# Ternary quantisation with interleaved groups on VectorE alone, and keys copied ahead

## What is computed

```
def _L0_attn_ref(x, Wq, Wk, Wv, Wo, lambda_init):      # 16 heads of 128
    q1, q2 = (q[..., :HHD], q[..., HHD:]); k1, k2 = (k[..., :HHD], k[..., HHD:])
    attn1 = softmax(causal(q1 k1^T * SCALE)); attn2 = softmax(causal(q2 k2^T * SCALE))
    out = (attn1 - lam * attn2) @ v
    return out.reshape(b, t, H * HD) @ Wo

def ternary_quant(w_fp32, g=64):
    w = w_fp32.astype(jnp.bfloat16)
    w_g = w.reshape(-1, g)
    scale = jnp.clip(jnp.mean(jnp.abs(w_g), axis=-1, keepdims=True), 1e-08, None)
    q = jnp.clip(jnp.round(w_g / scale), -1, 1)
    w_hat = (q * scale).reshape(w.shape)
    return w + jax.lax.stop_gradient(w_hat - w)

def _L0_ffn_ref(x, w_gate_up, w_proj):                 # 4096 x 512 and 512 x 2048
    gate, up = jnp.split(x @ ternary_quant(w_gate_up).T, 2, axis=-1)
    return rms_norm(silu(gate) * up) @ ternary_quant(w_proj).T
```

## Time and profile before

| | before |
|---|---|
| median of 3 runs | 1418.46 us (1415.54 to 1429.39) |
| span of the profiled execution | 1416.6 us |
| PE, PEld busy in it | 1114.3 us (79%), 825.4 us (58%) |
| DVE, ACT, POOL busy in it | 764.6, 469.9, 479.1 us (54%, 33%, 34%) |
| mean granted TensorE clock | 0.805 of full speed |

### The profile page before, as it was taken

How to read it: one execution, slowest core, us unless ns; L and a number is a source line. 1 busy time by engine, 2 the same in 40 slices (tenths; PEclk the granted TensorE clock), 3 DMA queues, 4 the chain that set the end, 5 groups by cost and what they waited for, 6 DMA issues and landing times.

```text
span 1416.6 us, 14414 instructions
## 1 busy us (share of the span) xinstructions
PE 1114.3 (79%) x5107; PEld 825.4 (58%) x5111; DVE 764.6 (54%) x1025; ACT 469.9 (33%) x719; POOL 479.1 (34%) x331
## 2 busy tenths in 40 slices
PE   3899977879999887686769689699733478489996
PEld 2543454547777766575657678544521367378885
DVE  6212122653344554998999995414697764533333
ACT  2111122552111634464446533333311132133331
POOL 5231212330000433465646560034454980011211
PEclk9799986975555897788878889899955555599999
DMA  6576601220000114313231300102030000111110
GB/s 174 204 266 215 253 0 28 58 60 19 0 0 1 56 42 157 117 47 119 74 106 58 125 10 16 60 0 74 15 121 0 0 0 1 48 60 44 59 44 30
DMA packets 50448, 97.88 MB, mean 69 GB/s; under 512 B 6796, under 2 KB 26564, under 8 KB 47838
## 3 DMA queue, kind: packets, MB, share of 16 engines
q1 hardware_dynamic: 47198, 86.59, 18.4%
q0 software_dynamic: 3200, 10.62, 2.2%
HBM read 96.14 MB, written 1.05 MB: 69 GB/s over the span
## 4 chain that ended last, share of the span: by engine, by line
PE 58%; DVE 23%; issue 11%; ACT 4%; POOL 2%; SPq 0%; DMA 0%; POOLq 0%; DVEq 0%; ACTq 0%
PE banks L41 7%; PE banks L42 7%; PE banks L43 7%; PE banks L354 6%; PE banks L1794 4%; PE banks L1097 3%; PE banks L1096 3%; PE banks L2109 2%; PE banks L1424 2%; PE banks L1452 2%; DVE da_a L1357 1%; PE banks L1087 1%; PE banks L1806 1%; DVE da_s L1351 1%; DVE da_s L1341 1%
## 5 line engine op out<-in xcount | busy, mean ns | idle before, releaser
L155 POOL TENSOR_TENSOR w_low<-w_raw,w_high 128x1024 fp32r<-128x1024 f32 (+2 forms) x66 | 129.9, 1982 | 307.9 <-ACT w_high L151 307.8
L354 PE MATMUL banks<-cs_rows,cs_col 128*2 128x512 f32 x192 | 85.3, 594 | 0.2 <-DVE w_raw L318 0.2
L1642 POOL TENSOR_TENSOR tw_abs<-tw_abs,tw_w 128x2048 bf16<-128x2048 bf16 x12 | 49.0, 4083 | 95.0 <-DVE tw_abs L1635 95.0
L151 ACT CAST w_high<-w_raw 128x1024 fp32r<-128x1024 f32 (+2 forms) x66 | 53.4, 831 | 83.2 <-DMA w_raw<-in_L_attn_Wq 47.1
L2217 POOL TENSOR_TENSOR hf_hl<-hf_h,hf_hh 128x512 fp32r<-128x512 f32 x16 | 20.6, 1289 | 155.1 <-ACT hf_hh L2271 155.1
L1424 PE MATMUL banks<-da_k,da_q 64*128 64x128 f32 x256 | 35.7, 396 | 38.4 <-issue 38.4
L1424 PEld LDWEIGHTS banks<-da_k,da_q 64*128 64x128 f32 x256 | 33.9, 288 | 41.5 <-issue 41.5
L41 PE MATMUL banks<-da_xT_high,w_high 128*128 128x512 f32 x128 | 52.5, 410 | 6.3 <-POOL w_low L155 5.7
L929 DVE SCALAR_TENSOR_TENSOR wa_s<-banks,wa_bd 128x288 f32<-128x288 f32 x16 | 7.3, 457 | 86.4 <-PE banks L1097 86.4
L41 PE MATMUL banks<-hf_xhh,w_high 128*128 128x512 f32 x128 | 51.7, 404 | 0.0
L669 POOL TENSOR_TENSOR wa_kr<-wa_kr,wa_tab 128x288 f32<-128x288 f32 x8 | 6.4, 794 | 132.8 <-ACT wa_kr L724 132.5
(11 more groups left out here) (419 smaller groups left out, 3160.7 us busy)
## 6 DMA issues: line engine op xcount, KB each, us to landing
cs_rows<-in_ctx SPq DMA_DIRECT2D x16, 1536.0 KB
tw_raw<-in_L_ffn_w_gate_up SPq DMA_DIRECT2D x32, 256.0 KB, 3.7
w_raw<-in_L_xattn_W_o SPq DMA_DIRECT2D x8, 512.0 KB
w_raw<-in_L_attn_Wq SPq DMA_DIRECT2D x8, 512.0 KB
w_raw<-in_L_attn_Wk SPq DMA_DIRECT2D x8, 512.0 KB
w_raw<-in_L_attn_Wv SPq DMA_DIRECT2D x8, 512.0 KB
w_raw<-in_L_attn_Wo SPq DMA_DIRECT2D x8, 512.0 KB
tw_raw<-in_L_ffn_w_proj SPq DMA_DIRECT2D x16, 256.0 KB, 3.8
```

Of the source, the lines that this page charges most:

```text
L151: self.nc.scalar.copy(self.wh[k][:, 0:cols], self.raw[k][:, 0:cols]).then_inc(self.split_hi[k], 1)
L155: self.nc.gpsimd.tensor_tensor(self.wl[k][:, 0:cols], self.raw[k][:, 0:cols], self.wh[k][:, 0:cols].bitcast(F32), ALU.subtract).then_inc(s ...
L354: ins = nc.tensor.matmul(out, self.col[:, h * self.HALF + r, :], self.rows[h][:, r, :], start=(h == 0 and r == 0), stop=False)
L1642: g.tensor_tensor(a, a, self.w[j][:, :], ALU.subtract).then_inc(self.d_ok, 1)
```

## The change

There are three parts.

1. The groups are interleaved. Within each quarter of a tile (512 elements, 8 groups of 64) the element k of group g goes to place 8 k + g. The cast on ACT writes it that way (reading on, writing with a step of 8 elements, 16 bytes). The broadcast then has its zero step in the middle and 8 neighbouring bf16 values innermost. The sum over a group reads with a step of 16 bytes. As the contracted features are now in another order, LayerNorm writes xn in that order for this block (a step of 32 bytes), and tw.out of w_gate_up writes guT with a step of 16 bytes, since the hidden features are contracted with w_proj, whose order is changed too. The threshold is now half the scale, in bf16.
2. The last two operations of a step leave POOL for DVE, in bf16 as before. The semaphores hat_ok and d_ok go.
3. A step on DVE has two parts: part 0 is the reduction, the two small operations and the comparison; part 1 is the multiplications by the scale and by the sign, the subtraction and the addition. The keys of the next round are copied between part 0 and part 1 of step j = 1. DVE's rounds are all written out.

```
-            if self.cast(n) is not None:
-                for j in range(2):
-                    self.tw.gpsimd(pool, i, j, n == 0)
...
-        def round_(i, n):
-            first = n == 0
+        def copy_keys(i, first):
             for h in range(2):
                 dve.wait_ge(self.proj, 8 * i + 3 + h)
                 if not first:
                     dve.wait_ge(self.s_done, 2 * i)
                 v.tensor_copy(self.k[:, h, :], c.bank[:, h, :]).then_inc(self.k_out, 1)
+
+        def round_(i, n):
+            first = n == 0
+            if first:
+                copy_keys(i, True)
...
             if self.cast(n) is not None:
-                self.tw.vector(dve, ch, i, 0, first)
+                for part in range(2):
+                    self.tw.vector(dve, ch, i, 0, first, part)
             for h in range(2):
                 dve.wait_ge(self.o_hi, 2 * i + h + 1)
                 v.tensor_tensor(self.ol[h][:, :], c.bank[:, 3 + 2 * h, :], self.oh[h][:, :].bitcast(F32), ALU.subtract).then_inc(self.o_lo, 1)
             if self.cast(n) is not None:
-                self.tw.vector(dve, ch, i, 1, first)
-        ch.per = 24
-        for a, b in self.SEGMENTS:
-            if b - a == 1:
-                round_(a, a)
-            else:
-                ch.loop(a, b, lambda i: round_(i, a))
+                self.tw.vector(dve, ch, i, 1, first, 0)
+            if n < PAIRS - 1:
+                copy_keys(i + 1, False)
+            if self.cast(n) is not None:
+                self.tw.vector(dve, ch, i, 1, first, 1)
+        for n in range(PAIRS):
+            round_(n, n)
...
-            nc.scalar.copy(self.w[j][:, :], self.raw[:, :]).then_inc(self.cast, 1)
+            by_group = self.w[j][:, :].rearrange("p (q k g) -> p q g k", q=4, k=GROUP)
+            nc.scalar.copy(by_group, self.raw[:, :].rearrange("p (q g k) -> p q g k", q=4, k=GROUP)).then_inc(self.cast, 1)
...
+    def vector(self, dve, ch, i, j, first, part):
...
+        by = lambda t: t.rearrange("p (q k g) -> p q k g", q=4, k=GROUP)
+        wide = lambda t: t[:, :].rearrange("p (q g) -> p q g", q=4).unsqueeze(2).broadcast_to([P, 4, GROUP, self.GR // 4])
+        if part == 0:
+            dve.wait_ge(self.cast, 3 * s + 2)
+            ch(v.tensor_reduce(self.sum[:, 0, :].rearrange("p (q g) -> p q g", q=4), a.rearrange("p (q k g) -> p q g k", q=4, k=GROUP), AX.X, ALU.add))
+            ch.wait()
+            ch(v.tensor_scalar(self.scale[:, :], self.sum[:, 0, :], 1.0 / GROUP, 1e-8, ALU.mult, ALU.max))
+            ch.wait()
+            ch(v.tensor_scalar(self.half[:, :], self.scale[:, :], 0.5, None, ALU.mult))
+            ch.wait()
+            ch(v.tensor_tensor(by(a), by(a), wide(self.half), ALU.is_gt))
+            return
+        ch.wait()
+        ch(v.tensor_tensor(by(a), by(a), wide(self.scale), ALU.mult))
         ch.wait()
         dve.wait_ge(self.cast, 3 * s + 3)
-        v.tensor_tensor(a, a, self.sg[j][:, :], ALU.mult).then_inc(self.hat_ok, 1)
-
-    def gpsimd(self, pool, i, j, first):
-
-        g, s = self.c.nc.gpsimd, i * 2 + j
-        pool.wait_ge(self.hat_ok, s + 1)
-        a = self.ab[j][:, :]
-        g.tensor_tensor(a, a, self.w[j][:, :], ALU.subtract).then_inc(self.d_ok, 1)
-        pool.wait_ge(self.d_ok, s + 1)
+        ch(v.tensor_tensor(a, a, self.sg[j][:, :], ALU.mult))
+        ch.wait()
+        ch(v.tensor_tensor(a, a, self.w[j][:, :], ALU.subtract))
+        ch.wait()
         if not first:
-            pool.wait_ge(self.t_done, 2 * (s - 1))
-        g.tensor_tensor(self.q[j][:, :], self.w[j][:, :], a, ALU.add).then_inc(self.q_ok, 1)
+            dve.wait_ge(self.t_done, 2 * (s - 1))
+        v.tensor_tensor(self.q[j][:, :], self.w[j][:, :], a, ALU.add).then_inc(self.q_ok, 1)
...
             if rows:
-                ins = nc.scalar.copy(self.guT[:, 2 * h:2 * h + 2, bass.ds(s * 512, 512)], src.rearrange("p (c n) -> p c n", c=2))
+                to = self.guT[:, 2 * h:2 * h + 2, bass.ds(s * 512, 512)].rearrange("p c (k g) -> p c g k", k=GROUP)
+                ins = nc.scalar.copy(to, src.rearrange("p (c g k) -> p c g k", c=2, k=GROUP))
...
-        self.ln = LayerNorm(core, self.to)
+        self.ln = LayerNorm(core, self.to, interleaved=True)
```

More of the change, by code:

```diff
@@ L171, with __init__ @@
 class LayerNorm:
-    def __init__(self, core, to, transposed=True, x=None):
-        self.to, self.x = to, core.x if x is None else x
+    def __init__(self, core, to, transposed=True, x=None, interleaved=False):
+        self.to, self.x, self.interleaved = to, core.x if x is None else x, interleaved
         self.c, self.u, self.transposed = core, core.lns, transposed
@@ L195, in vector @@
         for m in range(M):
-            nc.vector.tensor_scalar(self.to.xn[:, m, :], self.x[:, m, :], c.mv[:, m, 0:1], c.std[:, 2, m:m + 1],
+            xn, x = self.to.xn[:, m, :], self.x[:, m, :]
+            if self.interleaved:
+                xn, x = xn.rearrange("p (k g) -> p g k", k=GROUP), x.rearrange("p (g k) -> p g k", k=GROUP)
+            nc.vector.tensor_scalar(xn, x, c.mv[:, m, 0:1], c.std[:, 2, m:m + 1],
                                     ALU.subtract, ALU.mult).then_inc(c.ln_xn, 1)
@@ L1583, in __init__ @@
         self.scale = sb("scale", [P, self.GR], BF16)
-        self.thr = sb("thr", [P, self.GR], F32)
+        self.half = sb("half", [P, self.GR], BF16)
         sem = lambda name: core.sem("tw_" + name)
         self.raw_in = sem("raw_in")
-        self.cast, self.hat_ok, self.d_ok, self.q_ok, self.t_done, self.t_out = (sem(n) for n in ("cast", "hat", "d", "q", "t_done", "t_out"))
+        self.cast, self.q_ok, self.t_done, self.t_out = (sem(n) for n in ("cast", "q", "t_done", "t_out"))
     def load(self, sp, i, j, rows, first):
@@ L1615, in scalar @@
             nc.scalar.activation(self.sg[j][:, :], self.w[j][:, :], ACT.Sign).then_inc(self.cast, 1)
-    def vector(self, dve, ch, i, j, first):
+    def vector(self, dve, ch, i, j, first, part):
         v, s = self.c.nc.vector, i * 2 + j
-        dve.wait_ge(self.cast, 3 * s + 2)
-        by = lambda a: a.rearrange("p (g k) -> p g k", k=GROUP)
-        wide = lambda a: a.unsqueeze(2).broadcast_to([P, self.GR, GROUP])
-        ch(v.tensor_reduce(self.sum[:, 0, :], by(self.ab[j][:, :]), AX.X, ALU.add))
-        ch.wait()
-        ch(v.tensor_scalar(self.scale[:, :], self.sum[:, 0, :], 1.0 / GROUP, 1e-8, ALU.mult, ALU.max))
-        ch.wait()
-        ch(v.tensor_scalar(self.thr[:, :], self.scale[:, :], 257.0 / 512.0, None, ALU.mult))
-        ch.wait()
-        a = self.ab[j][:, :]
-        ch(v.tensor_tensor(by(a), by(a), wide(self.thr[:, :]), ALU.is_gt))
-        ch.wait()
-        ch(v.tensor_tensor(by(a), by(a), wide(self.scale[:, :]), ALU.mult))
+        a = self.ab[j][:, :]
+        by = lambda t: t.rearrange("p (q k g) -> p q k g", q=4, k=GROUP)
[10 more added lines that the diff above has]
+            return
+        ch.wait()
+        ch(v.tensor_tensor(by(a), by(a), wide(self.scale), ALU.mult))
```

## The result

| kernel | median of its runs, us | lowest to highest | span of the profiled execution, us |
|---|---|---|---|
| before, on the same chips | 1423.93 | 1415.54 to 1429.88 (4 runs) | 1416.6 |
| changed | 1506.31 | 1502.48 to 1510.74 (4 runs) | 1502.7 |

The changed kernel is slower by 6.1%: ratio 1.0611, 95% interval 1.0563 to 1.0659. (The ratios in this text are those on record with the runs. They are not the quotient of the two medians, here 1.0579, and differ from it by up to 0.6%.) The forecast was 1395 us, 1.6% faster, so it has the wrong sign, and the time lies far outside its range.

A forecast was written before the change was run, and what follows sets the result against it. DVE was taken to bound rounds 0 to 5. Savings of 13.0 us (A to T) and 12.1 (T to A), less 1.8 for LayerNorm, made 23.3: span 1416.6 to 1393.3, median 1395 us, range 1382 to 1420.

The forecast's parts named there:

- Strided accesses: New strides on ACT and DVE, priced from 64-byte-step rows: cast 1.9 to 3.8 us, tw.out 0.98 to 1.95, reduction 2.28 to 3.7.
- three signs of being wrong: PE's gap only moves to q's copy; DVE waits over 2 us ahead of the keys; strided prices off by over factor two.
- Slower: ACT becomes the bound: Rival, chance 0.10: ACT's queue between transposes and q's copy sets the pace once one tw.out reaches 2.7 to 3.0 us.
- The rival's own formula: ACT's copy of q in round 3 comes at A + 9.5 + 4d, d being the time of one tw.out.
- The rival's 1452 us: ACT's writes at four times dense (tw.out 3.8 us, cast 7.6): 28 and 18 us lost, 12 gained; chance 0.10.
- The half A to T: From DVE's end of a round's last L1357 (A) to the next round's first L1336 (T): 13.0 us saved in all.
- The half T to A: Softmax half, DVE's first L1336 to last L1357: 15.8 us in rounds 1 to 6 with POOL's splits only, 12.1 saved.
- The contention stays: Rival, chance 0.16: POOL's splits meet as many DVE operations in the softmax half, nothing of 12.1 us gained: 1407 us.
- LayerNorm: Strided write of xn: four writes end 2.3 us later than their 1.92, of which some 1.8 reach the first xT_low.
- The early keys: Next round's keys copied inside DVE's second quantisation step: PE's idle time ahead of the scores falls from 38.4 to under 10 us.

The follow-up runs named there:

- e1: The changed kernel with ACT's two strided writes (cast and tw.out) made dense, so its output differs: 1379.04 us, ratio to before 0.9736.
- e4: The changed kernel, same layout and output, with ACT's strides on the reading side and dense writes in cast and tw.out: 1384.27 us, ratio to before 0.9751.
- e8: The kernel before with POOL's two operations moved to DVE and the next round's keys copied early, groups not interleaved: 1399.16 us, ratio 0.9814.
- e5: The kernel before with only the early key copies inside the second quantisation step, POOL's operations kept, nothing interleaved: 1424.76 us, ratio 1.0047.
- e9: The changed kernel with strided reads and dense writes on ACT, groups interleaved in blocks of four: 1384.5 us, ratio to before 0.9748.

## Why the prediction was wrong

**The step that failed** is in "Strided accesses": "I take these prices: cast 1.9 to 3.8 us, tw.out 0.98 to 1.95 each". They measured 9.39 and 4.94 us, two and a half times the upper ends. The rows that I took them from, L746 and L915, are four-byte writes, and I scaled them by element. I wrote that "a write of 2 bytes might also cost more than one of 4", and yet put the upper end of the range at the four-byte price. With a term this open, a row of another element size was no bound. The prediction's three signs of being wrong all came: PE's gap moved to the copy of q, DVE waits some 13 us ahead of the keys in rounds 2 to 5, and the strided prices are off by more than a factor of two. The price decided the sign, as e1 and e4 show: my rival "Slower: ACT becomes the bound" named the place and the turning point, d = 2.7 to 3.0 us for one tw.out, and got 0.10.

**The rival's own formula** gives q at A + 9.5 + 4 x 4.7 = A + 28.3; it came at A + 34.2. What the formula left out is that the long cast of step 1 also stands ahead of the transposes' copies (L1291 at A + 10.4, the first tw.out at A + 11.3 instead of A + 3.9), 7.4 us; the rival priced it apart, at 3 to 3.7 us a round. The other way go some 1.5 us of waits in ACT's old queue that the long one no longer has. PE's projection of k then took 7.8 us where I had 5.5: PE had been idle for 6.1 us, the eight matmuls behind the first took 0.63 us each against 0.39 later, and the granted clock of that stretch was 0.72, a mix of the levels of 1.2 and 2.4 GHz.

```profile
664.53 0.80 PE L41 MATMUL banks<-da_xT_high,w_high 128*128 128x512 f32 x1 [6.09 <-ACT da_q L1266]
665.12 0.63 PE L42 MATMUL banks<-da_xT_low,w_high 128*128 128x512 f32 x1
...
671.97 0.40 PE L43 MATMUL banks<-da_xT_high,w_low 128*128 128x512 f32 x1
```

The rival's 1452 us took the strided writes at four times the dense price, with 46 us lost between A and T and 12 gained between T and A. Measured were 84.0 lost and 0.9 lost. The 38 us more between A and T go with the fifth multiple, the longer delay by the cast of step 1 and this lower clock, whose shares no run separates; the 12.9 between T and A are the waits for the exponentials and the late splits.

**The half A to T.** With the writes dense (e1) it is 181.0 us over seven rounds, 11.7 less than before, and in e4, whose cast has the price that I took, 179.2, 13.5 less; I had 13.0. The double rate of the comparison and the multiplication held (1225 and 1220 ns), so did the reduction (3.85 against my 3.7). PE's idle time ahead of the scores went from 38.4 us to none in the changed kernel and to 12.4 in e1. What bounds this half next was not what I had worked out. In e1 DVE finds both keys ready in rounds 1 to 6 and is idle for 0.5 us between A and T, so its own work is the bound. Only with the cast at 3.9 us (e4) does it wait for the second key, 0.3 to 1.8 us in rounds 1 to 5.

**The half T to A.** I took round 0's 15.8 us for all rounds and saved 12.1. With the writes dense it fell to 13.5 us in rounds 1 to 6, 27.1 saved in all (122.7 to 95.5). Counted above the shortest operation of the same line, DVE's operations had stretched by 43.2 us in these halves before and stretch by 17.0 in e1, which is 26.2 of it. In e8's round 3 POOL has two splits for 4.72 us in the softmax half, where round 0 before had three for 7.52; 6.0 us of POOL's work fall behind A. The case "The contention stays" is refuted, and of the saving I had counted less than half. In the changed kernel ACT's long casts took this gain back: the attention weights, queued behind a ternary load that waits for the cast, come late, and with them ACT's exponentials (DVE waits 20.4 us for them) and POOL's splits, which take 7.1 to 7.8 us of the softmax half in rounds 0 to 5.

**LayerNorm.** L199, an f32 write with a step of 8 values, takes 2.45 us for four against 1.92 dense, 0.5 us more instead of 2.3, of which the sum took 1.8. My row for it, L915, reads from the banks. No run here isolates the difference.

**The early keys.** I priced them together with the move from POOL, and rightly only together: e5 shows that alone they lose. Their value in my forecast rested on POOL being free, which the text said of the contention but not of the keys.

## What to carry to other kernels

A layout change moves cost to whoever writes the layout. Before it is priced, find a row with the same element size and the same side (read or write); if there is none, the range is open upward (here five times dense), and one run of the bare operation closes it. Ask also what waits behind a longer operation: here a cast held back a load, the load the weights, and the weights the exponentials. If a copy must permute, put the strides on its reading side and write dense: same values, same place, 9.4 us against 3.9 from SBUF, 4.7 against 1.0 from PSUM. And of two edits that each look good, test the pair and the singles: the keys ahead of time cost 0.5% alone (interval 0.1 to 0.9%) and gain 19 us from T to T once POOL's operations are gone.

## What the runs showed of the hardware that was not expected

- A bf16 write on ACT with a step of 1, 2, 4, 8, 16 values took 1.90, 2.46, 4.75, 9.25, 8.75 us for 2048 values, an f32 write 1.04, 1.10, 1.99, 2.02, 1.90 us for 1024. Per value and beyond dense, the two-byte write at a step of 8 costs 3.6 ns and the four-byte write 0.96. With two four-byte values in each 16 bytes (a step of 2) the write is nearly at the dense time, 1.10 against 1.04; with four two-byte values (also a step of 2) it is not, 2.46 against 1.90.
- POOL shows the same price as ACT (9.25 us), DVE half of it (4.70).
- ACT reads bf16 from PSUM with a step of 64 values at the dense time, 1.01 us for 1024.
- DVE's operations of two bf16 inputs keep 1.22 us for 2048 values with a zero step in the middle of the access and unit-step runs of 8 (the change) or 4 values (e9).
- DVE's bf16 reduction costs 2.29 us at steps 1, 2 and 4, and 3.73 at 8.
